# Neighbourhood attention beside global attention: strip values in two halves, keys and queries of a block placed five slots earlier, the head mask applied by GpSimd

## The chip, the cores and the metric

The kernel runs on one core of one Trainium2 chip, in one launch for eight images. The metric is the device time of that launch in microseconds; lower is better. Engines are named as the profile names them: PE is TensorE (PEld its weight loads), DVE VectorE, ACT ScalarE, POOL GpSimd, SP SyncE, which here only issues DMAs.

## The reference

Each image has 128 channels and 56 x 56 pixels. The first layer is a neighbourhood attention: after a group norm, each pixel of each of 16 heads attends to the 7 x 7 pixels around it, with a relative position bias. The second is a full attention over the 3136 pixels with 8 heads, between two layer norms, and the third a 128 x 128 product with a dequantised weight.

```python
x = x + _L0_conv_ref(_gn(x), ...)        # 7x7 neighbourhood attention, 16 heads of 8
t = _to_tokens(x)
t = t + _L1_attn_ref(_ln_t(t), ...)      # softmax over 3136 keys, 8 heads of 16
t = t + _L1_ffn_ref(_ln_t(t), ...)       # y @ W, W = dequantised nf4 times W
```

## The kernel before

While PE, ACT and DVE compute the full attention of image b, the same engines compute the first layer of image b+1 beside it, in small tasks. Only the first layer of image 0 runs alone, at the start (`front_alone`, some 489 us), and only the attention of image 7 runs without such tasks beside it.

**The main work.** An image's attention is 14 units (2 groups of 4 heads by 7 blocks of 448 queries), and a unit has 25 chunks of 128 keys. A chunk is a *slot*; an image has 350 of them, numbered t = 0 to 349, so image b begins at slot 350 b. In each slot PE makes four score products (`scores_turned`, line 1198, into three PSUM banks in turn), ACT takes their exponentials (line 1425), PE weighs the chunk before it with the values (`weigh`, line 1213), and PE and DVE find the row maxima of the next unit: PE makes scores again (`max_tile`, line 1149), DVE reduces them (line 1670), over three more banks.

**The tasks beside it** are placed by the class `Plan`, which gives each a slot and a half: (t, 0) comes behind the first of the slot's four score products, (t, 1) behind the third, after `weigh`. All engines walk the same plan in order, each doing its part of a task. Those that need PSUM all use one bank, the side bank, so there is one such task per half slot, and PE waits before each until the reader of the one before (named in `SIDE_READER`) has read the bank. `fix` puts a task at a given place; `place` takes the first free half slot from t on.

**A strip** is two pixel rows; an image has 28 of them, strip s at t = 39 + 9 s, so one per 9 slots. Its tasks: the rows of keys are copied by POOL at (t-5, 1) (`roll_keys`, line 825), the queries are spread by POOL at (t-4, 0) (`spread_queries`, line 848, two of 1.7 us), PE makes the scores at t, t+1 and t+2 (line 1016), DVE adds the bias, takes maxima (t+3), POOL subtracts (t+4, line 872), ACT takes exponentials (t+5, 1; line 1290), POOL adds the two halves of the keys (t+6, `halve_sum`, line 854), DVE sums them (t+7, 0; `sum_up`, line 1557) and inverts, POOL normalises (t+8, 1; line 878). PE turns the weights in four tasks (t+12 to t+15, half 0; line 1023), which ACT copies to `PT` (line 1296). At (t+17, 0), PE makes the strip's values (`values`, line 1032: 14 units of four 32-column products, which the profile records as 112 matmuls), from `PT` and from `VP`, which SP loads. ACT reads the bank four times, once for each of the 4 heads that share a partition group, multiplying by a column of `head_mask` (line 1304). POOL's `gather` at (t+17, 1) adds head pairs twice (lines 862 and 866) into `On`.

**A block** is 8 pixel rows, four strips; an image has 7. Keys and queries of block j need a normalised input (`norm`, DVE, line 1523), one product each (`k1`, read by DVE, line 1529, and `q1`, read by ACT, line 1284). `roll_keys` of strip 4 j - 2 is the first that needs the keys of block j: it waits on POOL for `k1_read`. Behind the values of a block's last strip come `proj`, `mean2`, `var2`, `k2`, `q2`, `v2` and their copies and splits, placed one behind the other from t = 39 + 9 (4 j + 5). Tasks of the attention's own units have fixed places in each unit of 25 slots: `spread` at 1, `project` at 3, `mean3` at 5, `var3` at 7, `ffn` at 10 (read by DVE, line 1616) and `turn_max` at 21, all in half 1 (`mean3`, `var3` and `ffn` in units 0 and 8 to 13).

Of the kernel before, what the change touches and what calls it, by code (L numbers as in the profile page):

```python
# [12 lines left out]
ALU = mybir.AluOpType  # L13
# [67 lines left out]
def max_keys(m):  # L81
# [12 lines left out]
BLOCK_ROWS = BLK // SIDE  # L94

SIDE_READER = {"gn_mean": "dve", "gn_var": "act", "k1": "dve", "v1": "act", "q1": "act", "scores": "dve",
               "turn": "act", "values": "act", "proj": "dve", "mean2": "dve", "var2": "act", "k2": "act",
               "q2": "act", "v2": "dve", "spread": "act", "project": "dve", "mean3": "dve", "var3": "act",
               "ffn": "dve", "turn_max": "act", "first_max": "dve", "combine": "dve"}

# [1 line left out]
class Plan:  # L102

    def __init__(self, front, attention):
        self.at, self.taken = collections.defaultdict(list), {}
        if attention:
            self.tails(attention)
        if attention in ("first", "middle", "last"):
            for k in range(AUNITS):
                t = k * CHUNKS  # L110
                if k < AUNITS - 1 or attention != "last":
                    self.fix(t + MAX_CHUNKS, 1, "turn_max", k + 1)
                    self.fix(t + MAX_CHUNKS, 1, "negate_max", k + 1)
                    self.fix(t + MAX_CHUNKS + 1, 1, "split_max", k + 1)
                    self.fix(t + MAX_CHUNKS + 2, 0, "send_shift", k + 1)
                if k < AUNITS - 2 or attention != "last":
                    self.fix(t + 2, 0, "load_q", k + 2)
            if attention != "first":
                for n in range(len(K_PARTS)):
                    self.fix(4 + 10 * n, 1, "load_k1", n)  # L120
                self.fix(2, 0, "load_v", 1)
            self.fix(1, 1, "copy_x", 0)
            self.fix(14, 1, "copy_x", 1)
            if attention != "last":
                self.fix(4, 1, "load_x", 0)
                self.fix(17, 1, "load_x", 1)
        if front and attention:
            self.front()
        elif front:
# [26 lines left out]

    def place(self, t, task, i):
        sub = 0
        while (t, sub) in self.taken:
            t, sub = t + sub, 1 - sub  # L160
        self.fix(t, sub, task, i)
        return t

    def front(self):
# [4 lines left out]
        for s in range(STRIPS):  # L169
            t = FIRST_STRIP + PERIOD * s  # L170
            for n in range(3):
                self.fix(t + n, 0, "scores", 3 * s + n)
            self.fix(t + 3, 0, "maxima", s)
            self.fix(t + 4, 0, "subtract", s)
            self.fix(t + 5, 1, "exponentials", s)
            self.fix(t + 6, 0, "halve_sum", s)
            self.fix(t + 7, 0, "sum_up", s)
            self.fix(t + 2 * PERIOD - 1, 1, "gather", s)
            self.fix(t + 8, 0, "invert_strip", s)
            self.fix(t + 8, 1, "normalise", s)  # L180
            for c in range(4):
                self.fix(t + PERIOD + 3 + c, 0, "turn", 4 * s + c)
            self.fix(t + 2 * PERIOD - 1, 0, "values", s)
            self.fix(t - 5, 1, "roll_keys", s)
            self.fix(t - 4, 0, "spread_queries", s)
            self.fix(t + (PERIOD if s else 0), 0, "load_windows", s)
# [4 lines left out]
            t = self.place(25 + j, "v1", j)  # L191
            self.fix(t + 1, 1, "store_v1", j)
        for j in range(NBLK):
            t = FIRST_STRIP + (PERIOD * (BLOCK_STRIPS * j - 3) if j else -7)
            self.fix(t, 1, "norm", NBLK + j)
            t = self.place(t + 1, "k1", j)
            self.place(t, "q1", j)
# [163 lines left out]
def hybrid_block(nc, images, x, consts, qkv_wT, rpb, proj_wT, proj_b, Wq, bq, Wk, bk, Wv, bv, Wo, bo,  # L361
# [8 lines left out]
    with ExitStack() as ctx:  # L370
# [3 lines left out]
        def sem(name):  # L374
            return ctx.enter_context(nc.semaphore(name))
# [43 lines left out]
        SUMS = sb("SUMS", [P, 2, 16])  # L419
        PT = sb("PT", [P, UNITS, P])  # L420
        VP = sb("VP", [P, UNITS, P])
        PVM = sb("PVM", [P, GH, UNITS, QI * QJ])
        On = sb("On", [P, 2, BLK])
        XL, SQ, SD = sb("XL", [P, BLK]), sb("SQ", [P, BLK]), sb("SD", [P, BLK])
        k_full, q_full, rest = sb("k_full", [P, BLK]), sb("q_full", [P, BLK]), sb("rest", [P, BLK])
# [29 lines left out]
        keys_rolled = sem("keys_rolled")  # L455
        scores_in, biased, max_in, shifted, exps = (
            sem("scores_in"), sem("biased"), sem("max_in"), sem("shifted"), sem("exps"))
        sum_halved, paired = sem("sum_halved"), sem("paired")
        summed, inverted, normalised = sem("summed"), sem("inverted"), sem("normalised")
        turned, turned_read = sem("turned"), sem("turned_read")  # L460
        windows_in = [sem("windows_in0"), sem("windows_in1")]
# [337 lines left out]
        def _(pool):  # L799
# [13 lines left out]
            def side(b, ahead):  # L813
# [43 lines left out]
                def gather(s):  # L857
                    j, at = s // BLOCK_STRIPS, s % BLOCK_STRIPS * (QI * SIDE)
                    pool.wait_ge(masked, of(b, ahead, STRIPS, s + 1))
                    if s % BLOCK_STRIPS == 0:  # L860
                        wait(pool, proj_in, of(b, ahead, NBLK, j - 1))
                    G.tensor_tensor(PVM[:, 0:2, :, :], PVM[:, 0:2, :, :], PVM[:, 2:4, :, :], ALU.add).then_inc(paired, 1)  # L862
                    pool.wait_ge(paired, of(b, ahead, STRIPS, s + 1))
                    v = PVM.rearrange("p h u (i j) -> p h i u j", i=QI)
                    o = On[:, j % 2, at:at + QI * SIDE].rearrange("p (i u j) -> p i u j", i=QI, u=UNITS)
                    G.tensor_tensor(o, v[:, 0, :, :, :], v[:, 1, :, :, :], ALU.add).then_inc(out_strip, 1)

# [83 lines left out]
        def _(pe):  # L951
# [11 lines left out]
            def side(b, ahead):  # L963
# [60 lines left out]
                                                  strip_buffer(s, ahead)[:, u, :], ident)  # L1024
                    ins.then_inc(turned, 1)

                def values(s, bank):
                    pe.wait_ge(turned_read, of(b, ahead, 4 * STRIPS, 4 * s + 4))
                    pe.wait_ge(windows_in[s % 2], of(b, ahead, 16 * windows_loaded(STRIPS - 2 + s % 2), 16 * windows_loaded(s)))
                    for u in range(UNITS):  # L1030
# [4 lines left out]
                    ins.then_inc(pv_in, 1)  # L1035

                def proj(j, bank):
                    if ahead == 0 and j == 0:
# [53 lines left out]
                def do(task, i, bank):  # L1092
# [11 lines left out]
                        scores(i // 3, i % 3, bank)  # L1104
                    elif task == "turn":
                        turn(i // 4, i % 4, bank)
                    elif task == "values":
                        values(i, bank)
                    elif task == "proj":
# [69 lines left out]
            def image(b, kind):  # L1179
# [3 lines left out]

                def beside(t, sub):
                    if (t, sub) in plan.taken:
                        pe.wait_ge(*side_read(b, 1, *previous[0]))
                        do(*plan.taken[t, sub], SIDE_BANK)
                        previous[0] = plan.taken[t, sub]

                def scores_turned(k, c, h):  # L1190
# [68 lines left out]
        def _(act):  # L1259
# [5 lines left out]
            def side(b, ahead):  # L1265
# [33 lines left out]
                def values(s, bank):  # L1299
                    act.wait_ge(pv_in, of(b, ahead, STRIPS, s + 1))  # L1300
                    wait(act, out_strip, of(b, ahead, STRIPS, s))
                    pv = PS[:, bank, 0:BLK].rearrange("p (u h q) -> p h u q", u=UNITS, h=GH)
                    for h in range(GH):
                        ins = S.activation(PVM[:, h, :, :], pv[:, h, :, :], ACT.Copy, scale=head_mask[:, h:h + 1])  # L1304
                    ins.then_inc(masked, 1)

                def square2(j):
# [438 lines left out]
```

## Time and profile before

| what | us |
|---|---|
| median of 3 runs | 8969.56 (8964.04 to 8975.93) |
| the profiled execution, its time | 8970.16 |
| the profiled execution, its span | 8968.4 |
| PE busy | 8560.5 (95%) |
| DVE busy | 7382.0 (82%) |
| ACT busy | 6653.4 (74%) |
| POOL busy | 2833.8 (32%) |

The span is what lies between the first and the last instruction of the profiled execution. Shares are of the span. On PE, the records of two matmuls can overlap, since they are pipelined; the step from the start of one group to the start of the next says better what a group costs.

### The profile page before, as it was taken

The numbers are of one execution on the slowest core, as the hardware profiler recorded it, in microseconds if no ns is written. First come the engines' busy times: TensorE is split into PE (matmuls) and PEld (weight loads), VectorE is DVE, ScalarE is ACT, GpSimd is POOL, SyncE is SP. The second block draws the span as 40 slices with busy tenths as digits, with TensorE's granted clock in tenths as the row PEclk, the third lists the DMA queues.
The fourth block names the chain that finished last, engine by engine and source line by source line (L and its number), as shares of the span: only waits on it lengthen the run. The fifth ranks groups of instructions, "written<-read, shape, count | busy, mean of one in ns | idle before, by whom it ended". The sixth has DMA issues, their size and how long they took to land.

```text
span 8968.4 us, 389859 instructions
## 1 busy us (share of the span) xinstructions
PE 8560.5 (95%) x173512; PEld 4493.3 (50%) x173512; DVE 7382.0 (82%) x12442; ACT 6653.4 (74%) x14241; POOL 2833.8 (32%) x2805
## 2 busy tenths in 40 slices
PE   5789999999999999999999999999999999999998
PEld 3445544555445554455554554545555455445543
DVE  5578888888788887888878887888878888789985
ACT  2367777777777777777777777777777777778877
POOL 5514431244412443034330444304442144420000
PEclk8899999999999999999999999999999999999999
DMA  1120101201011010110002001020101200011000
GB/s 45 35 55 21 27 19 28 48 19 28 26 39 30 21 28 24 43 29 20 25 26 54 19 23 26 24 52 17 26 26 28 48 16 24 26 28 31 9 10 8
DMA packets 312025, 253.99 MB, mean 28 GB/s; under 512 B 97244, under 2 KB 303052, under 8 KB 308300
## 3 DMA queue, kind: packets, MB, share of 16 engines
q1 hardware_dynamic: 310348, 229.05, 10.5%
q8 instruction: 1367, 22.40, 1.1%
q14 instruction: 310, 2.54, 0.1%
HBM read 136.82 MB, written 78.05 MB: 24 GB/s over the span
## 4 chain that ended last, share of the span: by engine, by line
PE 83%; DVE 5%; issue 5%; ACT 3%; POOL 2%; DMA 1%; SPq 0%; POOLq 0%; ACTq 0%; DVEq 0%
PE PS L1213 22%; PE PS L1149 22%; PE PS L1198 20%; PE PS L959 6%; PE PS L1016 5%; PE PS L1023 4%; PE PS L1032 2%; DVE block_max L1670 2%; ACT PB L1425 1%; PE PS L1008 1%; ACT tail L1343 1%; DVE NM L1548 1%; PE PS L991 0%; PE PS L1062 0%; POOL SC L872 0%
## 5 line engine op out<-in xcount | busy, mean ns | idle before, releaser
L1670 DVE TENSOR_REDUCE block_max<-PS 128x1 f32<-128x512 f32 (+1 forms) x9632 | 6132.2, 683 | 988.3 <-PE PS L1149 915.2
L1425 ACT ACTIVATE PB<-PS 128x448 f32<-128x448 f32 (+1 forms) x11200 | 5369.2, 546 | 1472.6 <-PE PS L1198 1451.9
L1198 PE MATMUL PS<-QP,KP 99*32 99x448 bf16 x43904 | 4313.0, 354 | 70.1 <-ACT PB L1425 43.4
L1149 PE MATMUL PS<-KP,QP 96*32 96x512 bf16 (+1 forms) x43904 | 4010.1, 355 | 34.6 <-issue 25.2
L1213 PE MATMUL PS<-PB,VA 128*32 128x448 f32 x22400 | 2703.1, 540 | 8.9 <-issue 7.3
L1198 PEld LDWEIGHTS PS<-QP,KP 99*32 99x32 bf16 x43904 | 1412.2, 97 | 1287.8 <-issue 484.7
L1149 PEld LDWEIGHTS PS<-KP,QP 96*32 96x32 bf16 x43904 | 1289.0, 96 | 1459.5 <-issue 537.1
L1213 PEld LDWEIGHTS PS<-PB,VA 128*32 128x32 f32 x22400 | 787.6, 111 | 398.0 <-issue 14.1
L872 POOL TENSOR_TENSOR SC<-SC,NM 128x1120 f32<-128x1120 f32 x210 | 432.8, 2061 | 1749.1 <-DVE NM L1548 1749.1
L848 POOL TENSOR_TENSOR QB<-Qn,C 128x896 f32<-128x896 f32 x392 | 661.2, 1706 | 11.9 <-ACT Qn L1284 11.9
L894 POOL CAST shift_parts<-shift 14x128 bf16<-14x128 f32 x112 | 31.3, 280 | 1773.7 <-ACT shift L1336 1773.7
L1296 ACT ACTIVATE PT<-PS 80x512 f32<-80x512 f32 (+1 forms) x896 | 479.3, 540 | 149.3 <-PE PS L1023 148.4
L1016 PE MATMUL PS<-KR,QB 128*32 128x80 f32 x21952 | 545.9, 234 | 27.6 <-DVE VS L1587 5.8
L1016 PEld LDWEIGHTS PS<-KR,QB 128*32 128x32 f32 x21952 | 474.9, 109 | 165.1 <-DVE VS L1587 27.6
L1539 DVE TENSOR_TENSOR SC<-PS,nat_bias 128x80 f32<-128x80 f32 (+3 forms) x1050 | 370.4, 386 | 189.2 <-PE PS L1016 89.2
L1023 PE MATMUL PS<-C,SC 128*80 128x128 f32 x2940 | 484.8, 283 | 37.2 <-ACT SD L1315 9.4
L1023 PEld LDWEIGHTS PS<-C,SC 128*80 128x80 f32 x2940 | 271.7, 119 | 381.0 <-issue 223.1
L862 POOL TENSOR_TENSOR PVM<-PVM 128x224 f32<-128x224 f32 x224 | 148.5, 663 | 936.7 <-ACT PVM L1304 936.0
L878 POOL TENSOR_TENSOR SC<-SC,SUMS 128x1120 f32<-128x1120 f32 x210 | 433.2, 2063 | 0.8
L854 POOL TENSOR_TENSOR HS<-SC 128x560 f32<-128x560 f32 x196 | 271.2, 1384 | 390.0 <-ACT SC L1290 390.0
L907 POOL TENSOR_TENSOR normed<-tail 128x448 f32<-128x448 f32 x112 | 127.8, 1141 | 691.5 <-ACT tail L1345 691.5
L1304 ACT ACTIVATE PVM<-PS,C 128x112 f32<-128x112 f32 x896 | 243.1, 354 | 119.7 <-PE PS L1032 119.3
(114 smaller groups left out, 4714.7 us busy)
## 6 DMA issues: line engine op xcount, KB each, us to landing
QP<-q_dram SPq DMA_DIRECT2D x672, 56.0 KB, 2.1
VP<-vT_padded SPq DMA_DIRECT2D x448, 70.0 KB
k_dram<-k_parts SPq DMA_DIRECT2D x56, 336.0 KB, 3.0
KP<-k_dram SPq DMA_DIRECT2D x336, 56.0 KB, 2.1
q_dram<-q_parts SPq DMA_DIRECT2D x56, 336.0 KB, 2.7
KP<-k_dram SPq DMA_DIRECT2D x48, 392.0 KB, 6.1
VA<-v_dram SPq DMA_DIRECT2D x16, 816.0 KB, 4.5
vT_padded<-SC SPq DMA_DIRECT2D x112, 112.0 KB
```

Source lines behind the costliest of these rows:

```text
L848: ins = G.tensor_tensor(dst, src, m, ALU.mult)
L872: G.tensor_tensor(sc, sc, m, ALU.add).then_inc(shifted, 1)
L878: G.tensor_tensor(sc, sc, r, ALU.mult).then_inc(normalised, 1)
L959: ins = mm(PS[at:at + 32, bank, 0:n], weights[:, at:at + 32], rhs, start=True, stop=True, tile_position=(0, at))
L1016: ins = mm(PS[r, bank, (u - u0) * KEYS:(u - u0 + 1) * KEYS], QB[:, u, r], KR[:, :, u * QJ:u * QJ + WJ], start=True, stop=True, tile_positi ...
L1023: ins = nc.tensor.transpose(PS[0:KEYS, bank, (u % 4) * P:(u % 4 + 1) * P], strip_buffer(s, ahead)[:, u, :], ident)
L1149: ins = mm(PS[at:at + QT, bank, n * width:(n + 1) * width], QP[0:ROWS, Q_SLOTS[k % AUNITS], t:t + QT], KP[0:ROWS, g, t // BLK, keys], star ...
L1198: ins = mm(PS[k0:k0 + 32, bank, 0:BLK], KP[0:ROWSM, k // NBLK, h, c * P + k0:c * P + k0 + 32], QP[0:ROWSM, Q_SLOTS[k], h * BLK:(h + 1) * B ...
L1213: ins = mm(PS[32 * h:32 * h + 32, SUM_BANK, 0:BLK], VA[:, g, at:at + 32], exp_buffer(k, c)[:, h, :], start=(c == 0), stop=(c == CHUNKS - 1 ...
L1296: S.activation(PT[0:KEYS, u0:u1, :].rearrange("p u e -> p (u e)"), PS[0:KEYS, bank, 0:(u1 - u0) * P], ACT.Copy).then_inc(turned_read, 1)
L1425: S.activation(exp_buffer(k, c)[0:n, h, :], PS[0:n, at % ST_BANKS, 0:BLK], ACT.Exp, scale=float(ADIM) ** -0.5).then_inc(exp_done, 1)
L1670: V.tensor_reduce(block_max[:, k % 2, queries.start:queries.stop, j], tile, AX.X, ALU.max).then_inc(max_read, 1)
```

## The change

Three edits. The values of a strip are made in two halves: seven units in slot t+16 (`early_values`), seven in t+17 (`late_values`), the second without a wait for the side bank's reader, since nobody reads between them; the half slot (t+16, 1) is kept free, and where an attention task already has it, the values stay whole. The keys and queries of blocks 1 to 6 are placed from five slots earlier on. And ACT copies the values' bank in one plain copy, with `PVM` laid out in the bank's own order; POOL multiplies it by the head mask before its two additions, in a multiplication of its own with its own semaphore. The first layer of image 0, alone at the start, keeps ACT's four masked reads, now into the new order.

```diff
+        self.at, self.taken, self.kept = collections.defaultdict(list), {}, set()
@@ place
-        while (t, sub) in self.taken:
+        while (t, sub) in self.taken or (t, sub) in self.kept:
@@ front, for each strip s at t
-            self.fix(t + 2 * PERIOD - 1, 0, "values", s)
+            u = t + 2 * PERIOD - 2
+            if (u, 1) not in self.taken:
+                self.fix(u, 0, "early_values", s)
+                self.kept.add((u, 1))
+            self.fix(u + 1, 0, "values", s)
@@ front, for each block j
-            t = FIRST_STRIP + (PERIOD * (BLOCK_STRIPS * j - 3) if j else -7)
+            t = FIRST_STRIP + (PERIOD * (BLOCK_STRIPS * j - 3) - 5 if j else -7)
             self.fix(t, 1, "norm", NBLK + j)
             t = self.place(t + 1, "k1", j)
             self.place(t, "q1", j)
@@ buffers
-        PVM = sb("PVM", [P, GH, UNITS, QI * QJ])
+        PVM = sb("PVM", [P, UNITS, GH, QI * QJ])
@@ POOL, gather
-                    G.tensor_tensor(PVM[:, 0:2, :, :], PVM[:, 0:2, :, :], PVM[:, 2:4, :, :], ALU.add).then_inc(paired, 1)
+                    if ahead:
+                        m = head_mask.rearrange("p (o h a) -> p o h a", o=1, a=1).to_broadcast([P, UNITS, GH, QI * QJ])
+                        G.tensor_tensor(PVM[:, :, :, :], PVM[:, :, :, :], m, ALU.mult).then_inc(own_kept, 1)
+                        pool.wait_ge(own_kept, of(b, 0, STRIPS, s + 1))
+                    G.tensor_tensor(PVM[:, :, 0:2, :], PVM[:, :, 0:2, :], PVM[:, :, 2:4, :], ALU.add).then_inc(paired, 1)
@@ PE
+                def weighed(units, bank):
+                    for u in units:
...
+                def early_values(s, bank):
+                    pe.wait_ge(turned_read, of(b, ahead, 4 * STRIPS, 4 * s + 4))
+                    pe.wait_ge(windows_in[s % 2], of(b, ahead, 16 * windows_loaded(STRIPS - 2 + s % 2), 16 * windows_loaded(s)))
+                    weighed(range(UNITS // 2), bank)
+
+                def late_values(bank):
+                    weighed(range(UNITS // 2, UNITS), bank).then_inc(pv_in, 1)
@@ PE, beside
                     if (t, sub) in plan.taken:
-                        pe.wait_ge(*side_read(b, 1, *previous[0]))
-                        do(*plan.taken[t, sub], SIDE_BANK)
+                        if previous[0][0] == "early_values":
+                            do("late_values", previous[0][1], SIDE_BANK)
+                        else:
+                            pe.wait_ge(*side_read(b, 1, *previous[0]))
+                            do(*plan.taken[t, sub], SIDE_BANK)
                         previous[0] = plan.taken[t, sub]
@@ ACT, values
+                    if ahead:
+                        S.activation(PVM.rearrange("p u h q -> p (u h q)"), PS[:, bank, 0:BLK],
+                                     ACT.Copy).then_inc(masked, 1)
+                        return
                     pv = PS[:, bank, 0:BLK].rearrange("p (u h q) -> p h u q", u=UNITS, h=GH)
                     for h in range(GH):
-                        ins = S.activation(PVM[:, h, :, :], pv[:, h, :, :], ACT.Copy, scale=head_mask[:, h:h + 1])
+                        ins = S.activation(PVM[:, :, h, :], pv[:, h, :, :], ACT.Copy, scale=head_mask[:, h:h + 1])
```

## Rows read from the trace of the kernel before

**Rows 1.** Busy us (xinstructions) of PE, PEld, DVE, ACT, POOL; clock; DMA: third image.
```profile
2656.00:3744.00 1088.00, 1062.67 (x21703) 552.40 (x21696) 914.48 (x1547) 832.13 (x1781) 363.78 (x353) 1.00 0.12 29
```

**Rows 2.** Waits of PE: us in total, times, longest.
```profile
PE PS L1198 <- ACT PB L1425: 43.4, 103, 1.2
PE PS L1032 <- DVE X L1616: 29.8, 7, 4.3
...
PE PS L1032 <- issue: 15.6, 25, 2.2
...
PE PS L1213 <- issue: 7.3, 8, 2.2
...
PE PS L1023 <- ACT Qn L1284: 7.0, 7, 1.0
```

**Rows 3.** The same columns, slot 236 of seven images: the third, and the sum.
```profile
3397.10:3408.30 11.20, 6.94 (x164) 3.29 (x160) 5.30 (x10) 3.41 (x9) 4.65 (x5) 0.70 0.11 36
...
sum 76.50, PE 46.67 PEld 22.87 DVE 37.32 ACT 24.34 POOL 31.96; mean PE 6.67 PEld 3.27 DVE 5.33 ACT 3.48 POOL 4.57
```

**Rows 4.** Timeline, PE, slot 236: start, us, what, xcount, [idle before].
```profile
3401.73 1.73 PE L1032 MATMUL PS<-PT,VP 96*32 96x32 f32 x112 [4.26 <-DVE X L1616]
...
3408.32 0.36 PE L1198 MATMUL PS<-QP,KP 99*32 99x448 bf16 x4
```

**Rows 5.** Timeline, DVE, slots 234 to 236.
```profile
3392.90 0.62 DVE L1529 COPY Kn<-PS 128x448 f32<-128x448 f32 x1 [0.91 <-PE PS L959]
...
3398.68 0.74 DVE L1557 TENSOR_REDUCE SUMS<-HS 128x14 f32<-128x560 f32 x1 [3.96 <-POOL HS L854]
...
3401.06 0.61 DVE L1616 TENSOR_TENSOR X<-X,PS 128x448 f32<-128x448 f32 x1
```

**Rows 6.** Timeline, POOL, the same slots.
```profile
3393.59 0.40 POOL L825 COPY KR<-Kn 128x56 f32<-128x56 f32 x2 [11.52 <-DVE Kn L1529]
3393.95 3.37 POOL L848 TENSOR_TENSOR QB<-Qn,C 128x896 f32<-128x896 f32 x2
3397.28 1.36 POOL L854 TENSOR_TENSOR HS<-SC 128x560 f32<-128x560 f32 x1
```

**Rows 7.** Waits of POOL from the first image on.
```profile
POOL KR L825 <- DVE Kn L1529: 221.6, 14, 20.7
```

**Rows 8.** Busy time and clock (after POOL) behind the stall of slot 236.
```profile
3401.70:3408.60 6.90, 6.87 (x160) 3.29 (x160) 2.58 (x5) 2.73 (x8) 3.10 (x3) 0.58 0.19 59
```

**Rows 9.** Timeline, all engines, an ordinary strip.
```profile
3000.58 0.93 PE L1213 MATMUL PS<-PB,VA 128*32 128x448 f32 x8
...
3001.34 0.36 PE L1198 MATMUL PS<-QP,KP 99*32 99x448 bf16 x4
...
3005.99 0.39 ACT L1296 ACTIVATE PT<-PS 80x256 f32<-80x256 f32 x1
...
3007.46 0.36 PE L1198 MATMUL PS<-QP,KP 99*32 99x448 bf16 x4
...
3009.90 0.36 PE L1198 MATMUL PS<-QP,KP 99*32 99x448 bf16 x4
...
3010.09 1.11 PE L1032 MATMUL PS<-PT,VP 96*32 96x32 f32 x110
...
3011.02 0.38 PE L1149 MATMUL PS<-KP,QP 96*32 96x512 bf16 x1
```

**Rows 10.** Timeline, PE, inside another strip's values.
```profile
2985.00 0.22 PE L1032 MATMUL PS<-PT,VP 96*32 96x32 f32 x2 [0.50 <-issue]
```

**Rows 11.** Groups by line and shape: busy us, mean ns, idle before.
```profile
L1304 ACT ACTIVATE PVM<-PS,C 128x112 f32<-128x112 f32 x896 | 243.1, 354 | 119.7 <-PE PS L1032 119.3
...
L907 POOL TENSOR_TENSOR normed<-tail 128x448 f32<-128x448 f32 x112 | 127.8, 1141 | 691.5 <-ACT tail L1345 691.5
...
L1408 ACT ACTIVATE tail<-PS 128x448 f32<-128x448 f32 x112 | 60.9, 544 | 63.6 <-PE PS L1213 62.8
```

**Rows 12.** Line 1579: min/median/max ns.
```profile
L1579 DVE TENSOR_TENSOR XL<-XL,SD x56: 615/616/1787, 138.2 to 7985.6; 128x448 f32<-128x448 f32 x56
```

More of the change, by code:

```diff
@@ L96 @@
 SIDE_READER = {"gn_mean": "dve", "gn_var": "act", "k1": "dve", "v1": "act", "q1": "act", "scores": "dve",
-               "turn": "act", "values": "act", "proj": "dve", "mean2": "dve", "var2": "act", "k2": "act",
+               "turn": "act", "values": "act", "early_values": "act", "proj": "dve", "mean2": "dve", "var2": "act", "k2": "act",
                "q2": "act", "v2": "dve", "spread": "act", "project": "dve", "mean3": "dve", "var3": "act",
@@ L104, in __init__ @@
     def __init__(self, front, attention):
-        self.at, self.taken = collections.defaultdict(list), {}
+        self.at, self.taken, self.kept = collections.defaultdict(list), {}, set()
         if attention:
@@ L457, in hybrid_block @@
             sem("scores_in"), sem("biased"), sem("max_in"), sem("shifted"), sem("exps"))
-        sum_halved, paired = sem("sum_halved"), sem("paired")
+        sum_halved, own_kept, paired = sem("sum_halved"), sem("own_kept"), sem("paired")
         summed, inverted, normalised = sem("summed"), sem("inverted"), sem("normalised")
@@ L861, in gather @@
                         wait(pool, proj_in, of(b, ahead, NBLK, j - 1))
-                    G.tensor_tensor(PVM[:, 0:2, :, :], PVM[:, 0:2, :, :], PVM[:, 2:4, :, :], ALU.add).then_inc(paired, 1)
+                    if ahead:
[3 more added lines that the diff above has]
+                    G.tensor_tensor(PVM[:, :, 0:2, :], PVM[:, :, 0:2, :], PVM[:, :, 2:4, :], ALU.add).then_inc(paired, 1)
                     pool.wait_ge(paired, of(b, ahead, STRIPS, s + 1))
-                    v = PVM.rearrange("p h u (i j) -> p h i u j", i=QI)
+                    v = PVM.rearrange("p u h (i j) -> p h i u j", i=QI)
                     o = On[:, j % 2, at:at + QI * SIDE].rearrange("p (i u j) -> p i u j", i=QI, u=UNITS)
@@ L1025, in turn @@
                     ins.then_inc(turned, 1)
[L1027 to L1030, printed above, removed]
+                def weighed(units, bank):
+                    for u in units:
                         for g in range(4):
@@ L1034, in values @@
                                      start=True, stop=True, tile_position=(0, 32 * g))
-                    ins.then_inc(pv_in, 1)
+                    return ins
+                def early_values(s, bank):
[4 more added lines that the diff above has]
+                    weighed(range(UNITS // 2, UNITS), bank).then_inc(pv_in, 1)
+                def values(s, bank):
+                    pe.wait_ge(turned_read, of(b, ahead, 4 * STRIPS, 4 * s + 4))
+                    pe.wait_ge(windows_in[s % 2], of(b, ahead, 16 * windows_loaded(STRIPS - 2 + s % 2), 16 * windows_loaded(s)))
+                    weighed(range(UNITS), bank).then_inc(pv_in, 1)
                 def proj(j, bank):
@@ L1106, in do @@
                         turn(i // 4, i % 4, bank)
+                    elif task == "early_values":
+                        early_values(i, bank)
+                    elif task == "late_values":
+                        late_values(bank)
                     elif task == "values":
```

## The prediction

> **What bounds the kernel now.** I read the share of busy time first, then the stretches by image, then what PE waited for, and last the timeline of the one slot that these waits pointed to. In the third image's attention PE is busy 1062.7 of 1088.0 us, DVE 914, ACT 832, POOL 364 [rows 1]. So PE's own stream is the bound; another engine matters only where it makes PE stand still, and all that can be won is such standing and what follows it. An image has 350 slots, so a slot is 3.1 us on average.
>
> PE's waits [rows 2] hold one entry that is not spread out: values (line 1032) waiting for DVE's line 1616, 29.8 us in 7 times, at most 4.3, so 4.26 in each of seven images. It is in slot 236, where the values of strip 20 follow the read of `ffn`. That slot takes 11.2 us in the third image and 76.5 us over the seven images [rows 3]; the reader sees there that PE is busy only 46.7 of them, and that its clock is granted at 0.70.
>
> The chain behind it can be followed back. The values start at 3401.73 after 4.26 us of nothing [rows 4]; DVE's line 1616 starts at 3401.06, behind the sum of strip 21 (line 1557) at 3398.68, for which DVE stood 3.96 us waiting for POOL [rows 5]. POOL had waited 11.52 us for the keys of block 6 (line 1529), and then had the copy, 3.37 us of `spread_queries` and `halve_sum` to do, in this order [rows 6]. The keys came at 3392.90 [rows 5], since their task stood in (234, 1), while the copy that needs them stood in (232, 1). Such a wait was there in every image: 14 waits of POOL for line 1529, 221.6 us [rows 7], of which seven of this kind would be 81.
>
> While PE stands, its clock falls: in the 6.9 us behind the stall the granted clock is 0.58 of 2.4 GHz on average [rows 8], near its lower level of 1.2 GHz, and work that needs 4.0 us takes 6.9. So one stall costs some 4.3 us of standing and 2.9 us of slow work.
>
> **Keys and queries five slots up.** By the plan's own rule, `norm` of block 6 was at 39 + 9 (24 - 3) = 228; from 229 on, the half slots were held by the scores of strip 21, `proj` 4, `mean3`, the turns of strip 20, `mean2`, `var3`, `var2`, and the first free one was (234, 1). Now it starts at 223, and (224, 1) is free: block 6's keys come in slot 224, eight before they are needed. Blocks 1 to 5 had their keys 3, 2, 1, 2 and 2 slots ahead and get 8, 8, 8, 8 and 8: nothing to win there. The work itself only moves.
>
> What goes is the excess of slot 236. Its own work: the values 0.93 us (3010.09 to 3011.02), four products of line 1198 at 0.19 (3009.90 to 3010.09), four of line 1149, 512 columns instead of 448, at 0.22, one of line 1213 at 0.76 (3000.58 to 3001.34) and `k2` of the same shape, 0.76 [rows 9]. That is 4.1, over seven images 29. The seven slots took 76.5 [rows 3], so the excess is 48; I leave 2 for ordinary small waits. Term: **-46 us**, and its bounds are -43 and -48, since the wait is the same in all seven and only its aftermath varies. The first layer of image 0, alone at the start, is placed by another function and keeps its time.
>
> Against it: `q1` and `k1` now come among the turns instead of among the scores. ACT has the strip's exponentials and the turns' copies there, and PE waits for `q1`'s reader half a slot later. The row for such a wait is line 1023 waiting for line 1284: 7.0 us, 7 times, so one per image of up to 1.0 us [rows 2]. Now `q1` stands directly ahead of a turn, a half of values or scores in all six blocks; block 1's `norm` stands half a slot ahead of its `k1`. I take **+3 us**, between -7 (that wait goes) and +14 (two more per image).
>
> **Values in two halves.** In 23 of 28 strips (not 19, 20, 22, 24 and 25, where half (t+16, 1) belongs to the attention); over seven images 161 times. The number of products is the same. What splits is a burst of 112 products in 0.93 us. PE stands inside it and just behind it "for issue": 15.6 us before line 1032 and 7.3 us before line 1213 [rows 2]; one case is a gap of 0.50 us before the last two of one strip [rows 10]. A burst of half the length may run out half as often. Bounds 0 and -23, I take a third, **-8 us**.
>
> The Trainium skill ("Runtime: NRT & Kernel Launch", Instruction fetch mechanics) says that fetching is hidden, because the sequencer dispatches more slowly than the fetch fills. By this the gaps are not fetches, or not ones that a shorter burst avoids, the term is 0, and the sum would give 8922 instead of 8914.
>
> A second entry into the burst could cost something. At its start nothing shows: the product before the values takes 0.19 us, as 448 columns do [rows 9]. But the burst needs 0.93 us where its columns, at 0.76 us per 448 in this type, come to 14 x 0.054 = 0.76. Were all the 0.17 at its ends, 161 more entries cost 27 us. Bounds 0 and +27; the start weighs more, so **+3 us**.
>
> A new wait could come in: the first half needs the last turned quarter in `PT` one slot sooner. In an ordinary strip ACT ends that copy at 3005.99 + 0.39 = 3006.38; the first half would follow the product that starts at 3007.46, so at 3007.65 [rows 9]. 1.27 us to spare: no cost. `VP`, loaded by SP from t+9 on, is 7 slots old. Behind an unsplit or late half, `q2` moves from (t+16, 0) to (t+17, 1), one slot later, and `v2` and their splits and stores with it; their users are in the next image, or, for `XL` and the side bank, half a slot away as before. I take nothing for it beyond the +3 above.
>
> **The mask.** ACT's four reads take 243.1 / 896 = 0.27 us each, 1.08 us a strip; a plain copy of 448 columns from PSUM takes 0.54 [rows 11]. ACT gains 0.54 us in 196 strips, 106 us, but PE is the bound. What PE waits for exponentials is 43.4 us in 103 waits in the whole run [rows 2]. Were they spread evenly, the values' slots, one in nine, would hold 5; they are the slots where ACT has most to do, so I take **-8 us**, between 0 and -25 (over half of that row). A loss is excluded on ACT, since nothing is added to it.
>
> POOL gets 196 multiplications of 448 columns: the nearest row is line 907 at 1.14 us [rows 11], so 223 us, 32 per image, hidden in 724 us per image in which POOL is idle [rows 1]. Behind it in POOL's queue stands `normalise` of the next strip, whose result PE needs three and a half slots later, 11 us, while the two additions, the multiplication and the normalising are under 5. If this cover were gone each strip would pay up to 1.1 us, 223 in all.
>
> The Trainium skill ("SBUF — State Buffer", SBUF: two separate sides) speaks against this edit: POOL and DVE share a port pair that is locked for a whole instruction when DVE reads two SBUF operands. The trace agrees: line 1579, with two such operands, takes 0.616 us at the median and 1.787 at most [rows 12].
>
> **The sum.** -46 + 3 - 8 + 3 - 8 = -56 us. Against the profiled execution's own 8970.2 us that is 8914; the median of the runs is 0.6 us lower, which changes nothing here. What is late next in slot 236 is PE itself.
>
> **Rivals.**
> 1. *The halves and the copy bring more.* ACT is behind PE in each values slot, and the gaps for issue go with the long burst. For it: both sit in the same slots. Against: the waits are few. -46 - 18 - 20 = -84, so 8886.
> 2. *Entries eat it.* Each added entry into fp32 products costs the 0.17 us: 27 instead of 3, and the waits for issue stay: -46 + 3 + 27 - 4 = -20, so 8950.
> 3. *The first half waits (slower).* ACT does its copy of the last turn later than 1.27 us behind, because the strip's exponentials and now `q1` come just ahead of it, and PE stands at (t+16, 0) in 161 places. From 0.35 us in each on, all of the 56 is gone; at 0.5 it costs 80, and the time is 8994. For it: ACT is busy 76% and that is its fullest stretch. Against: 1.27 us, and turns have a fixed rhythm.
> 4. *POOL's wait is only renamed*: the copy of the keys waits for another thing, the sum of strip 21 stays late, and only small terms are left: -8 or so, 8962. Against: POOL's wait is put down to line 1529 and nothing else stood ahead of it.
> 5. *The port lock.* If line 1579 (49 times beside attention) always met the multiplication, it would lose 1.787 - 0.616 = 1.17 us each, 57 us, all on the chain to `k2`: 8971. Against: it stands at (235, 0) for block 4, the multiplication one and a half slots later at (236, 1).
>
> **Chances.** Forecast 0.66 (its own range 8898 to 8930), rival 1 0.14, rival 2 0.10, rival 3 0.04, rival 4 0.04, rival 5 0.02. The range takes in the forecast, rival 1 with its bounds (-46 - 23 - 25 = -94, less a little) and rival 2: 8874 to 8954. A measurement of this kernel tells 0.2%, 18 us, from no change: faster is below 8952, that is the forecast, rival 1 and 0.09 of rival 2, 0.89; within it rivals 4 and 5 and the last 0.01 of rival 2, 0.07; slower rival 3, 0.04.
>
> **What would show it.** Right: POOL's wait of line 825 for line 1529 falls by about 80 us; no wait of line 1032 for line 1616 of 4 us; slot 236 takes 4 to 5 us at full clock. Of the copy: line 1304 has 308 instructions instead of 896, the new ones near 0.54 us; of the mask: 196 on POOL near 1.1 us. Of the halves: fewer waits of line 1032 for issue and none for line 1296. Wrong: an image's attention that takes over 1084 us, or a new PE wait that repeats by the strip.

## The result, and the profile after

The changed kernel takes 8890.24 us at the median of 4 runs (8888.70 to 8895.99), the kernel before 8971.36 (8964.04 to 8975.93) beside it: the ratio is 0.9912, with a 95% interval of 0.9894 to 0.9929, so 0.9% faster: 81 us between the medians, 79 by the ratio. The prediction said 8914 with 8874 to 8954; the result lies inside that range, but outside the forecast's own 8898 to 8930 and 4 us from rival 1's 8886. The profiled execution took 8895.99 us, its span is 8893.9.

The stall of slot 236 is gone. This is the view of [rows 3] for the changed kernel, the same slot of the seven images; columns as there. It takes 38.3 us instead of 76.5, for the same work (strip 20 is one of the five whose values stay whole), and the clock column is 1.00 in each of the seven.

```profile
3374.40:3381.10 6.70, 4.80 (x168) 2.54 (x160) 3.31 (x7) 2.77 (x6) 3.61 (x4) 1.00 0.19 58
...
sum 38.30, PE 31.38 PEld 18.15 DVE 23.87 ACT 20.32 POOL 16.41; mean PE 4.48 PEld 2.59 DVE 3.41 ACT 2.90 POOL 2.34
```

PE's waits, the view of [rows 2]. The 29.8 us for the read of `ffn` are 5.6, at most 0.8 each. Line 1038 is the old 1032, 1239 the old 1213, 1224 the old 1198. The waits for issue hardly moved at line 1038 and fell from 7.3 to 4.5 at 1239, from 25.2 to 18.6 at line 1172 (the old 1149) and from 7.3 to 2.9 at 1224. Line 1031's wait for `q1`'s reader ([rows 2]: line 1023 for line 1284, 7.0 us) is gone. Two waits are longer: the products of line 967 for `norm` (line 1553), 1.6 us before, and for POOL's gather (line 874), 2.6 before.

```profile
PE PS L1224 <- ACT PB L1455: 43.5, 94, 1.2
...
PE PS L1038 <- issue: 15.2, 23, 2.2
...
PE PS L967 <- DVE XN L1553: 7.1, 8, 1.6
...
PE PS L967 <- POOL On L874: 5.9, 7, 0.8
PE PS L1038 <- DVE X L1646: 5.6, 7, 0.8
...
PE PS L1239 <- issue: 4.5, 2, 3.6
```

POOL's wait for the keys, the view of [rows 7]: 81.4 us less, seven waits instead of 14.

```profile
POOL KR L829 <- DVE Kn L1559: 140.2, 7, 20.3
```

The new instructions, the view of [rows 11]: ACT's plain copy takes 0.545 us and POOL's multiplication 0.935, not 1.14.

```profile
L868 POOL TENSOR_TENSOR PVM<-PVM,C 128x448 f32<-128x448 f32 x196 | 183.2, 935 | 883.6 <-ACT PVM L1329 883.3
...
L1329 ACT ACTIVATE PVM<-PS 128x448 f32<-128x448 f32 x196 | 106.9, 545 | 22.0 <-PE PS L1038 21.2
```

One slot that the prediction had not looked at gained most beside 236: slot 245, where the values of strip 21 stood whole. Here it is in the kernel before, the third and fourth image and the sum of seven: 37.2 us, in the fourth image 6.8 us with the clock at 0.78.

```profile
3433.50:3439.10 5.60, 3.72 (x204) 2.45 (x200) 2.96 (x7) 3.21 (x9) 3.03 (x3) 0.93 0.12 31
4523.30:4530.10 6.80, 4.66 (x201) 2.80 (x197) 3.01 (x7) 3.19 (x9) 3.09 (x3) 0.78 0.09 26
...
sum 37.20, PE 26.10 PEld 17.86 DVE 20.51 ACT 21.94 POOL 17.88; mean PE 3.73 PEld 2.55 DVE 2.93 ACT 3.13 POOL 2.55
```

In the changed kernel half of the values (0.46 us of work, 3.3 in seven images) stand one slot earlier, and the seven slots take 22.0 us. So 12 us went here, and what PE had stood for was no engine: the gaps are put down to issue. The longest of the fourth image, before:

```profile
4527.32 0.35 PE L1149 MATMUL PS<-KP,QP 96*32 96x64 bf16 x11 [2.15 <-issue]
```

The changed kernel, fourth image and sum:

```profile
4484.10:4487.50 3.40, 2.81 (x147) 1.89 (x142) 2.51 (x6) 2.39 (x6) 1.77 (x3) 1.00 0.18 49
...
sum 22.00, PE 19.99 PEld 13.71 DVE 17.27 ACT 17.11 POOL 10.74; mean PE 2.86 PEld 1.96 DVE 2.47 ACT 2.44 POOL 1.53
```

### The profile page after: what moved, and what is told of

Same layout as the page of the kernel before. It is cut to its first block, busy times and chain, and to the rows that moved or that the text cites. A ratio compares the mean times of both kernels' runs of the same rounds, so it can differ in the third digit from the quotient of the medians.

```text
span 8893.9 us, 389467 instructions
## 1 busy us (share of the span) xinstructions
PE 8528.5 (96%) x173512; PEld 4534.7 (51%) x173512; DVE 7401.2 (83%) x12442; ACT 6567.1 (74%) x13653; POOL 3024.4 (34%) x3001
## 3 DMA queue, kind: packets, MB, share of 16 engines
q8 instruction: 1367, 22.40, 1.1%
## 4 chain that ended last, share of the span: by engine, by line
PE 86%; DVE 6%; ACT 3%; issue 3%; POOL 2%; DMA 0%; SPq 0%; POOLq 0%; ACTq 0%; DVEq 0%
PE PS L1239 23%; PE PS L1172 23%; PE PS L1224 20%; PE PS L967 7%; PE PS L1024 5%; PE PS L1031 4%; DVE block_max L1700 3%; PE PS L1038 2%; PE PS L1016 1%; ACT PB L1455 1%; ACT tail L1373 1%; DVE NM L1578 1%; PE PS L999 1%; PE PS L1081 0%; DVE X L1630 0%
## 5 line engine op out<-in xcount | busy, mean ns | idle before, releaser
L1224 PE MATMUL PS<-QP,KP 99*32 99x448 bf16 x43904 | 4307.2, 354 | 64.9 <-ACT PB L1455 43.5
L1172 PE MATMUL PS<-KP,QP 96*32 96x512 bf16 (+1 forms) x43904 | 3998.8, 355 | 26.4 <-issue 18.6
L868 POOL TENSOR_TENSOR PVM<-PVM,C 128x448 f32<-128x448 f32 x196 | 183.2, 935 | 883.6 <-ACT PVM L1329 883.3
L1038 PEld LDWEIGHTS PS<-PT,VP 96*32 96x32 f32 x25088 | 300.4, 110 | 112.9 <-issue 23.0
```

What stands on the lines that cost most here:

```text
L1038: ins = mm(PS[32 * g:32 * g + 32, bank, 32 * u:32 * u + 32], VP[0:KPAD, u, 32 * g:32 * g + 32], PT[0:KPAD, u, 32 * g:32 * g + 32], start=T ...
L1172: ins = mm(PS[at:at + QT, bank, n * width:(n + 1) * width], QP[0:ROWS, Q_SLOTS[k % AUNITS], t:t + QT], KP[0:ROWS, g, t // BLK, keys], star ...
L1224: ins = mm(PS[k0:k0 + 32, bank, 0:BLK], KP[0:ROWSM, k // NBLK, h, c * P + k0:c * P + k0 + 32], QP[0:ROWSM, Q_SLOTS[k], h * BLK:(h + 1) * B ...
```

## The experiments

All were timed in five rounds beside the kernel before, in three groups, each on a chip of its own; times are compared within a group or by the ratio to before.

**Group 1: each edit alone.** Its theory A was the prediction's.

```diff
+            t = FIRST_STRIP + (PERIOD * (BLOCK_STRIPS * j - 3) - 5 if j else -7)   # keys alone: this line only
```

> Of the three edits only the keys and queries of blocks 1 to 6 five slots up. Theory A (the wait of GpSimd in slot 236 is the largest single term, and more than half of the whole gain): slot 236 loses 5 to 6 us in each of seven images and block 1's keys, half a slot behind their norm, give back 1 us in each, so 30 to 42 us faster than before (0.4 to 0.5%). Rival B (the stall of that slot stays in part, since the four masked reads of ScalarE and the unsplit burst hold it too): under 20 us.

Measured: 8924.45 us against 8962.61, ratio 0.9956 (0.9944 to 0.9969): 38 us faster, theory A. Slot 236 takes 38.0 us in seven images, as in the changed kernel:

```profile
sum 38.00, PE 30.93 PEld 17.99 DVE 23.26 ACT 23.57 POOL 12.99; mean PE 4.42 PEld 2.57 DVE 3.32 ACT 3.37 POOL 1.86
```

```diff
# halves alone: the changed kernel with
-            t = FIRST_STRIP + (PERIOD * (BLOCK_STRIPS * j - 3) - 5 if j else -7)
+            t = FIRST_STRIP + (PERIOD * (BLOCK_STRIPS * j - 3) if j else -7)
# and without `if ahead:` in ACT's values and in POOL's gather
```

> Of the three edits only the values in two halves; the old layout of the keys, and ScalarE's four masked reads (into the new order of PVM). Theory A (long bursts make TensorE stand for issue, and the burst and the late reads behind it make ScalarE late): 15 to 30 us faster. Rival B (a second entry into the burst costs what the first half saves, and the gain of the values' slots is the mask's): within 8 us of before. Slot 236 keeps its 10 to 11 us in both.

Measured: 8924.75, ratio 0.9955 (0.9942 to 0.9967): 38 us faster. That is as much as the keys, and above theory A's range of 15 to 30. Slot 236 stays at 72.8 us of 76.5, slot 245 takes 20.3 instead of 37.2 (3.3 of it moved); the sums over seven images of this kernel, first of slot 236, then of slot 245:

```profile
sum 72.80, PE 42.97 PEld 22.70 DVE 37.49 ACT 24.25 POOL 31.81; mean PE 6.14 PEld 3.24 DVE 5.36 ACT 3.46 POOL 4.54
```
```profile
sum 20.30, PE 19.63 PEld 13.71 DVE 17.20 ACT 19.72 POOL 5.51; mean PE 2.80 PEld 1.96 DVE 2.46 ACT 2.82 POOL 0.79
```

```diff
# mask alone: the changed kernel with the keys' old line, and without
-            if (u, 1) not in self.taken:
-                self.fix(u, 0, "early_values", s)
-                self.kept.add((u, 1))
```

> Of the three edits only the plain copy by ScalarE with the mask applied by GpSimd. Theory A (ScalarE's 0.54 us per strip reach TensorE only through its few waits): 4 to 15 us faster. Rival B (the copy is what relieves the values' slots): 20 to 35 us faster. Rival C (GpSimd's multiplication delays what stands behind it): not faster.

Measured: 8965.86 against 8962.61, ratio 1.0004 (0.9995 to 1.0013): no difference, below theory A. PE's wait for POOL's gather ahead of `proj` is 5.9 us as in the changed kernel, 2.6 before:

```profile
PE PS L964 <- POOL On L871: 5.9, 7, 0.8
```

The fourth has the keys and the mask, without the three lines of the halves.

> The changed kernel without the halves: keys five slots up and the mask by GpSimd. If the edits add up, its gain is that of the keys alone and of the mask alone, some 45 us in theory A; what it lacks to the changed kernel's 80 is the halves' part, 25 to 35 us. Rival: the halves bring nothing once ScalarE's reads are one copy, then it is as fast as the changed kernel, 8890.

Measured: 8922.50, ratio 0.9953 (0.9941 to 0.9966), 40 us faster. The changed kernel's 79 exceed this by 39, just over the 25 to 35 expected for the halves, and the rival (8890) falls. So the edits add up: keys 38, halves 38, mask 0, together 76; all three were 79.

**Group 2: why the halves are worth 38 us.**

```diff
# moves only: the kernel before, with `kept` and its test in `place` as in the change, and with
-            self.fix(t + 2 * PERIOD - 1, 0, "values", s)
+            u = t + 2 * PERIOD - 2
+            if (u, 1) not in self.taken:
+                self.kept.update({(u, 0), (u, 1)})
+            self.fix(u + 1, 0, "values", s)       # whole
```

> The kernel before, with both half slots of slot t+16 held free in the 23 strips where the halves would stand, but the values whole at (t+17, 0). So q2, v2 and what follows them move exactly as with the halves, and nothing else does. The halves alone had brought 38 us. Theory A (the length of the burst is what costs): within 8 us of before. Rival B (the gain is that q2 and v2 no longer stand around the values and the scores): 20 us or more faster.

Measured: 8975.83 against 8962.44, ratio 1.0015 (1.0006 to 1.0023): 13 us slower. The moves of `q2` and `v2` cost something, so the split itself brings 38 and these 13, if the two add up. Rival B falls; so does "within 8 us", though only just.

```diff
# values twice: the kernel before with
-                    for u in range(UNITS):
+                    for u in list(range(UNITS)) * (2 if ahead else 1):
```

> The kernel before with each strip's burst of values made twice in a row in the images beside the attention (the same results written again): 56 more matmuls in 196 places. If TensorE's own speed in the burst is all, each place costs what its columns need, 0.76 us, or what the burst was seen to take, 0.93 us: 149 to 182 us slower. Theory A (behind the first dozens of matmuls the burst goes at the rate at which they are issued, and what follows has no lead): over 1.1 us in each place, more than 215 us slower. Rival B (engines behind TensorE catch up in the longer burst, so part is hidden): under 150 us.

Measured: 9708.23, ratio 1.0831 (1.0816 to 1.0845): 746 us slower, 3.8 us for each place, four times the 0.93 us that a burst was seen to take. Theory A holds; its bound was over 1.1 us a place. The timeline shows where: PE in one such burst. It begins at 3318.77 and goes on for 1.46 us; then PE is idle for 2.00 us in the middle of the burst, behind which also the next product, line 1213, takes 1.64 us instead of 0.93.

```profile
3317.16 0.93 PE L1213 MATMUL PS<-PB,VA 128*32 128x448 f32 x8
...
3318.77 1.46 PE L1032 MATMUL PS<-PT,VP 96*32 96x32 f32 x151
3322.24 0.80 PE L1032 MATMUL PS<-PT,VP 96*32 96x32 f32 x71 [2.00 <-issue]
...
3323.68 1.64 PE L1213 MATMUL PS<-PB,VA 128*32 128x448 f32 x8
```

Over the run there are 186 such standstills, nearly one in each of the 196 bursts:

```profile
PE PS L1032 <- issue: 315.6, 186, 2.6
```

What is missing are the instructions, as three things show. First, the count. On the page, the DMA queue of the kind "instruction" moves 1539 packets in this kernel and 1367 in the one before:

```profile
PE 8932.5 (92%) x195464; PEld 4762.9 (49%) x195464; DVE 7389.8 (76%) x12442; ACT 6670.4 (69%) x14241; POOL 2833.1 (29%) x2805
...
q8 instruction: 1539, 25.21, 1.1%
```

```profile
q8 instruction: 1367, 22.40, 1.1%
```

PE has 21,952 matmul records more, and as many weight loads: 43,904 in 172 packets more, 255 each, of 16.4 KB. Counted with PE's own semaphore waits, the kernel before has 350,163 records of PE and PEld in the trace and 1367 packets, 256 each. So PE's instructions come in blocks of 256 records. A strip's values are 224 of them in 0.93 us, nearly a block, and twice that in the doubled burst. Second, the place. I numbered PE's records, weight loads included, in the order of time and looked at where it stands for over 150 ns beyond what its columns need: of the standings over 600 ns in the doubled kernel, 225 of 333 lie in the same 8 of 256 places.

Third, the packets themselves, whose times are in the trace. In the doubled kernel nineteen in twenty of the standings over 600 ns at these places (216 of 228, counted from start to start of the matmuls) end 1.2 to 1.7 us after a packet of this queue has landed; of the standings elsewhere 25 of 178 do. In the kernel before it is 39 of 45 against 8 of 65. And in none of the fourteen kernels do two such packets start less than 3.2 us apart, though their own time is 1.0 us at the median.

The sum of standing within 5 records of that place, worked out so for each kernel (elsewhere 11 places hold some 14 us in the kernel before; the last column compares medians):

| kernel | standing at block ends, us | time against before, us |
|---|---|---|
| before | 80 | 0 |
| keys alone | 81 | -38 |
| mask alone | 73 | +3 |
| moves only | 87 | +13 |
| halves alone | 41 | -38 |
| changed kernel | 48 | -81 |
| values in three parts | 43 | -68 |
| whole burst in two slots | 252 | +335 |
| values twice in a row | 464 | +746 |

In the kernel before, blocks that PE used up in under 2.0 us (32 of them) ended in 0.96 us of standing on average, those of 2.0 to 2.5 us in 0.55, of 2.5 to 3.0 in 0.21, of 3.0 to 3.5 in 0.11, and those of 4 to 6 us in 0.01. So a block takes some 3 us to come, which fits the 3.2 us between packets, and PE is late only where it eats one faster than that.

```diff
# three parts: the changed kernel with
-                self.kept.add((u, 1))
+                self.fix(u, 1, "middle_values", s)
# and range(5), range(5, 10), range(10, UNITS) in the three, made in this order
```

> The changed kernel with the values in three parts, units 0 to 4 in (t+16, 0), 5 to 9 in (t+16, 1), which the halves leave empty, and 10 to 13 in (t+17, 0). Theory A (the shorter the burst, the less TensorE stands in and behind it): 5 to 20 us faster than the changed kernel's 8890, at 8870 to 8885. Rival B (a half is short enough, and each entry costs): as the changed kernel or up to 15 us slower.

Measured: 8894.69, ratio 0.9925 (0.9913 to 0.9938), beside 0.9912 for the changed kernel: no gain, rival B. It is 4 us slower by the medians and 12 by the ratios, whose intervals overlap. The standing at block ends is 43 instead of 48: what is left of it is elsewhere.

```diff
# mended: the changed kernel with
-            t = FIRST_STRIP + (PERIOD * (BLOCK_STRIPS * j - 3) - 5 if j else -7)
+            t = FIRST_STRIP + (PERIOD * (BLOCK_STRIPS * j - 3) - (5 if j > 1 else 0) if j else -7)
-            t = FIRST_STRIP + PERIOD * (BLOCK_STRIPS * (j + 1) + 1)
+            t = FIRST_STRIP + PERIOD * (BLOCK_STRIPS * (j + 1) + 1) + (j == NBLK - 1)
```

It rests on two places of the changed kernel. In slot 44 PE's `k1` of block 1 waits 0.79 us for its `norm`. That stands half a slot ahead now, a whole slot before, and it runs beside POOL's `spread_queries` (from 2756.49 on) and takes 1.15 us:

```profile
2757.30 1.15 DVE L1553 TENSOR_SCALAR XN<-X,gn 128x448 f32<-128x448 f32 x1
...
2758.59 0.96 PE L967 MATMUL PS<-XN,W_qkv 128*32 128x448 f32 x8 [0.79 <-DVE XN L1553]
```

And in slot 300 the last `proj` waits 0.84 us for POOL, whose gather begins with the new 0.94 us:

```profile
3581.39 0.94 POOL L868 TENSOR_TENSOR PVM<-PVM,C 128x448 f32<-128x448 f32 x1 [5.49 <-ACT PVM L1329]
...
3583.14 0.42 POOL L874 TENSOR_TENSOR On<-PVM 128x112 f32<-128x112 f32 x1
...
3583.71 0.96 PE L967 MATMUL PS<-On,W_proj 128*32 128x448 f32 x8 [0.84 <-POOL On L874]
```

> The changed kernel with two placements mended: block 1's keys and queries where they were before (their norm stands half a slot ahead of them now, and TensorE waits 1.0 us per image in slot 44), and the last block's proj one slot later (it waits for GpSimd's longer gather, 1.3 us per image in slot 300 against 0.6 before). Theory: 5 to 14 us faster than the changed kernel, 8876 to 8885. Rival (such waits are filled by others): no difference.

Measured: 8882.23, ratio 0.9911 (0.9896 to 0.9926). The median is 8 us below the changed kernel's, as theory has it, but it was timed in another group, beside a median of before that is 9 us lower; by the ratios, 0.9911 and 0.9912, there is no difference. Not settled. The waits themselves did go: PE's for `norm` in line 967 is 1.6 us again, not 7.1, and the one for POOL's gather, 5.9, is no longer in the list.

**Group 3: the block theory's own test, and the mask.**

```diff
# whole burst in two slots: the kernel with the halves alone, with
-                    weighed(range(UNITS // 2), bank)
+                    weighed(range(UNITS), bank)
-                    weighed(range(UNITS // 2, UNITS), bank).then_inc(pv_in, 1)
+                    weighed(range(UNITS), bank).then_inc(pv_in, 1)
```

> The kernel with the halves alone, but each half makes all 14 units: the whole burst of values in (t+16, 0) and once more in (t+17, 0), in 161 places (the five unsplit strips once). The same 56 added matmuls per place as in the kernel with the values made twice in a row, which cost 746 us, 3.8 us per place. Theory A (TensorE's instructions come in blocks of 256 records, and it stands where two blocks are used up faster than one arrives): 161 times 0.95 us for the work and the standing at block ends of about twice the 65 us of the kernel before, so 200 to 260 us slower than before, 1.2 to 1.6 us per place. Rival B (added matmuls cost what their issue costs, wherever they stand): 3.8 us per place, 610 us slower.

Measured: 9303.61 against 8969.01, ratio 1.0375 (1.0361 to 1.0389): 335 us slower, 2.1 us per place. It lies outside both ranges, nearer to A: the same added work costs 3.8 us in a row and 2.1 us a slot apart. A's account fits and its size was wrong: the standing at block ends is 252 us, 172 more than before and not 65, and with 161 x 0.95 = 153 for the work this makes 325 of the 335. Against the halves alone, on which it is built (ratio 0.9955), it is 377 us slower, 2.3 per place, with 211 more standing. B, with 610, falls. There are 110 standstills in the values, at most one per burst:

```profile
PE PS L1034 <- issue: 70.7, 110, 2.5
```

For the burst twice in a row the same account gives 384 us more standing and 182 for the work, 566 of 746. Its clock is lower as well, 0.969 against 0.985 in the kernel before, in the mean over the run, 1.6% of 9692 us, so at most 155 us, since part of the low clock lies in the idle time itself: after the 2.00 us of idling above, the product of line 1213 takes 1.64 us instead of 0.93, as work was slow behind the stall of slot 236 [rows 8]. At least 25 of the 746 us stay unexplained. Span and mean granted clock of the core, first with the burst twice in a row, then in the kernel before:

```profile
core 0: 9692.5 us, clock 0.969
```
```profile
core 0: 8968.4 us, clock 0.985
```

```diff
# the mended kernel without `if ahead:` in ACT's values and in POOL's gather
```

> The mended kernel (block 1's keys back, the last proj one slot later) with ScalarE's four masked reads instead of the plain copy and GpSimd's multiplication. Theory A (the mask's edit is worth nothing by itself, and what it lost at the last proj is mended): 0 to 10 us slower than the mended kernel, 8882 to 8892. Rival B (the edit costs): faster than 8880.

Measured: 8883.59 against 8969.01, ratio 0.9905 (0.9892 to 0.9919); the mended kernel had 0.9911. No difference that can be told: the mask's edit is worth nothing here either. It is in theory A's range by its time, while by the ratios it is the faster of the two.

```diff
# all strips halved: the mended kernel with
-            self.fix(u + 1, 0, "values", s)
+                self.fix(u + 1, 0, "values", s)
+            else:
+                self.fix(u + 1, 0, "early_values", s)
+                self.fix(u + 1, 1, "values", s)
```

> The mended kernel with the values of the five unsplit strips also in two halves, in (t+17, 0) and (t+17, 1), with k2 of block 4 one half slot on. Theory A (a burst of 224 records costs some 1.4 us of standing more than two halves: 38 us over 161 places is 0.24 us each, and more where a 64-column maximum tile or two fp32 products follow): 35 places, 5 to 15 us faster than the mended kernel's 8882. Rival B (half a slot between the halves is too little, and the reader comes later): no faster.

Measured: 8880.01, ratio 0.9901 (0.9888 to 0.9915), 3.6 us below the mended kernel with ScalarE's mask in the same group, from which it differs in the mask too; beside the mended kernel itself (0.9911) it is 9 us faster by the ratios, with intervals that overlap. The standing at block ends is 37 us, against 46 in the mended kernel. It goes the way of theory A, but neither comparison tells it from no change. Its median is the lowest of all, by a hair: 89 us below before.

```diff
# mask thrice: the mended kernel with
-                        G.tensor_tensor(PVM[:, :, :, :], PVM[:, :, :, :], m, ALU.mult).then_inc(own_kept, 1)
-                        pool.wait_ge(own_kept, of(b, 0, STRIPS, s + 1))
+                        for n in range(3):
+                            G.tensor_tensor(PVM[:, :, :, :], PVM[:, :, :, :], m, ALU.mult).then_inc(own_kept, 1)
+                            pool.wait_ge(own_kept, of(b, 0, 3 * STRIPS, 3 * s + n + 1))
```

> The mended kernel with GpSimd's multiplication by the head mask made three times (the mask is 0 and 1, so the result is the same): 1.9 us more on GpSimd in each of 196 places, 365 us in all. Theory A (GpSimd's cover is some 6 us in each strip): within 10 us of the mended kernel's 8882. Rival B (the wait for GpSimd's gather, seen ahead of proj, comes everywhere once it is longer): over 25 us slower.

Measured: 8907.22, ratio 0.9930 (0.9916 to 0.9943): 24 us slower than the same kernel without POOL's mask (8883.59), between the two theories. PE waits for POOL's gather 32 times, 16.0 us, ahead of `proj`, which accounts for two thirds of the 24; the strips' own `normalise` is not in the list of its waits. So POOL's cover is good in each strip, but not for the `proj` that follows the last strip of a block.

```profile
PE PS L968 <- POOL On L875: 16.0, 32, 0.6
```

## Why the prediction was right, and where its sizes were wrong

The direction and the range held; the forecast of -56 us was 23 short of -79, because one small term was large and another nothing. The result lies beside rival 1 and outside the forecast's own range, so the stated range held by the room that it gave to rival 1. And rival 1's 8886 is partly luck: it took 18 for the halves and 20 for the copy, where the halves brought 38 and the copy nothing.

- **Keys five slots up, -46 and +3.** Right in place, cause and nearly in size. The edit alone brought 38 us. Slot 236 fell from 76.5 to 38.0 us in seven images, 38.5; the 46 had left only 0.3 us per image for ordinary waits in that slot, and 1.4 stayed (5.5 us a slot at the full clock, where 4 to 5 were to show). GpSimd's wait fell by 81.4 us where 81 were named. Of the term against it, the wait for `q1`'s reader went (-7.0), and another came: block 1's `k1` behind its `norm`, in slot 44, where PE waits for `norm` 7.1 us in line 967 against 1.6 before (+5.5, 0.8 per image). Overlooked was what lengthens it. Each of the 42 norms that were moved now falls beside POOL's `spread_queries` and takes 0.77 to 1.87 us, where its median is 0.50 in either kernel: 25 us more on DVE, which shows in PE's waits in slot 44 alone. Line 1523 before, and the same line, 1553, in the changed kernel:

```profile
L1523 DVE TENSOR_SCALAR XN<-X,gn 128x448 f32<-128x448 f32 x112 | 69.6, 622 | 1.1 <-ACT gn L1271 1.0
```
```profile
L1553 DVE TENSOR_SCALAR XN<-X,gn 128x448 f32<-128x448 f32 x112 | 94.8, 847 | 1.1 <-ACT gn L1297 1.0
```

- **Values in two halves, -8 and +3.** The step that failed: "a burst of half the length may run out half as often. Bounds 0 and -23, I take a third." The mechanism was right as far as it went (it named no cause for the gaps), and half of the standing was indeed saved (80 us at block ends became 41 in the halves alone). The size was taken from PE's idle time put down to issue at two lines, 22.9 us [rows 2]. But a matmul's recorded end is modelled, and a busy record covers the first 0.2 to 0.4 us of a standing; and part of it came at other lines, such as the 64-column products of slot 245 (2.15 us, above). The sign that was named, fewer waits of line 1032 for issue, therefore did not show: 15.2 us after 15.6. With the cost of the moved `q2` and `v2`, 13 us, the split itself is worth some 51. What a second entry costs is not shown: with the values in three parts, and 5 us less of standing, the kernel came out 4 to 12 us slower, which does not clear the noise.
- **What fetching costs.** The Trainium skill ("Runtime: NRT & Kernel Launch", Instruction fetch mechanics) says that instructions come in blocks of 256 and that fetching is hidden. The first agrees with this case, 255 records per added packet. The second does not: standings end 1.2 to 1.7 us after an instruction packet has landed, with 80 us of standing at block ends before, 464 in the doubled burst. It would have given 8922.
- **The mask, -8.** Wrong: the edit alone gave +3 (-4 to +12 by its interval). ACT's half microsecond per strip did not reach PE; PE's waits for exponentials are 43.5 us as before, 43.4 [rows 2]. The cover for POOL's multiplication was argued for `normalise` and held there, but `proj` had been forgotten: it follows the gather of a block's last strip by half a slot in block 6 and by a whole one in most others, and PE's wait there went from 2.6 to 5.9 us, 7 times, once per image.
- **The rivals.** Rival 1 gave 8886 and its reasons were half right: half of the standing for instructions went, the copy brought nothing. Rival 2 priced each added entry at 0.17 us; the values in three parts add as many again, 27 us by its price, and were 4 to 12 slower. Rival 3's slower end did not come: line 1038 waits for the last turned quarter (line 1322) 2 times, 0.4 us in all, as line 1032 did for line 1296 before. Rival 4 is excluded by slot 236. Rival 5 was about line 1579 at (235, 0); a DVE instruction that takes longer beside POOL's work showed elsewhere, in the `norm` of the keys above.

## What to carry to other kernels

Where one engine's wait sits in a queue with other engines' work behind it, one misplaced task costs several times its own delay: look for a wait with a count equal to the number of outer iterations, and follow it back to what stood too late. And count TensorE's instructions as well as its columns: many small matmuls in a row can use up instructions faster than they arrive, which shows only as small gaps "for issue" spread over other lines; put other work, with long matmuls, between such bursts. An edit that relieves an engine which the bound engine does not wait for brings nothing.

## What the runs showed of the hardware

- TensorE's instruction stream arrives in blocks of 256 records (43,904 records more, 172 packets more). A block used up in under 2 us was followed by 0.96 us of standing, one of 4 to 6 us by 0.01. Two instruction packets never started less than 3.2 us apart, and 216 of 228 long standings at block ends of the doubled kernel ended 1.2 to 1.7 us after a packet had landed.
- 56 more small fp32 matmuls, whose columns need some 0.76 us by the estimate of the prediction, cost 3.8 us when they lengthen a burst of 56 and 2.1 us when they stand a slot away.
- The granted clock fell behind such gaps too: 6.8 us of slot 245 at 0.78 in the kernel before, and 0.969 over the whole run with the doubled burst, against 0.985.
- An fp32 TENSOR_SCALAR of 128x448 on VectorE took 0.50 us, and 0.77 to 1.87 us in each of the 42 places where it met GpSimd's TENSOR_TENSOR of 128x896.
